# Two graph layers on one core: the attention weight as the larger of two exponentials, the second written to PSUM in pieces

## The reference

```python
# layer 0: maximum over the first 25 neighbours
h = jnp.maximum(_layernorm(x, axis=-1), 0.0)
vals, idx = jax.lax.top_k(scores, S)                 # S = 25, scores = -index where adj != 0
agg = feats.max(axis=2)                              # feats: the rows idx of h
x = x + relu(concat(h, agg) @ W + b)
# layer 1: attention
h = jnp.maximum(_layernorm(x, axis=-1), 0.0) @ W1
s1, s2 = h @ a1, h @ a2
e = jax.nn.leaky_relu(s1[:, :, None] + s2[:, None, :], negative_slope=0.4)
att = jax.nn.softmax(jnp.where(adj > 0, e, -1e+20), axis=1)
x = x + gelu(einsum('bij,bjo->bio', att, h))
```

## Time and profile before

| | |
|---|---|
| median of three runs | 4289.62 us |
| the profiled execution | 4290.73 us, span 4288.9 us |
| first and last gather start | 31.1 and 4116.5 us |
| DVE busy | 3346.5 us (78%) |
| POOL busy | 3107.7 us (72%) |
| PE busy | 2657.1 us (62%) |
| ACT busy | 1947.6 us (45%) |

### The profile page before, as it was taken

How to read it: one execution, slowest core, us unless ns; L and a number is a source line. 1 busy time by engine, 2 the same in 40 slices (tenths; PEclk the granted TensorE clock), 3 DMA queues, 4 the chain that set the end, 5 groups by cost and what they waited for, 6 DMA issues and landing times. The chain is left out here.

```text
span 4288.9 us, 43562 instructions
## 1 busy us (share of the span) xinstructions
PE 2657.1 (62%) x13568; PEld 2016.8 (47%) x13568; DVE 3346.5 (78%) x7253; ACT 1947.6 (45%) x2108; POOL 3107.7 (72%) x3205
## 2 busy tenths in 40 slices
PE   2333356666666666675676666666666666666669
PEld 2222234554445454454454554455445554454547
DVE  5666689966898669986799767996689876998656
ACT  4223255532665236642366335553255532664146
POOL 5777777777777777777777777777777777777730
PEclk8555557677777777777767777777776777677779
DMA  6555556666666766666666766666666666566531
GB/s 216 166 167 173 174 183 216 209 221 212 208 213 206 232 212 197 218 221 223 203 216 204 226 222 206 213 199 225 213 211 217 210 225 218 188 218 202 172 114 55
DMA packets 412749, 860.09 MB, mean 201 GB/s; under 512 B 67299, under 2 KB 248422, under 8 KB 396134
## 3 DMA queue, kind: packets, MB, share of 16 engines
q0 software_dynamic: 153600, 419.64, 32.0%
q1 hardware_dynamic: 258918, 437.67, 30.2%
HBM read 714.43 MB, written 142.61 MB: 200 GB/s over the span
## 5 line engine op out<-in xcount | busy, mean ns | idle before, releaser
L410 POOL DMA_INDIRECT gb<-h_table,idx x3200 | 3107.0, 971 | 1009.2 <-issue 962.2
L965 PE MATMUL ps_av<-hz,lk 128*128 128x256 f32 x3712 | 1136.1, 474 | 179.1 <-DVE hz L805 179.1
L965 PEld LDWEIGHTS ps_av<-hz,lk 128*128 128x128 f32 x3712 | 891.4, 247 | 418.9 <-issue 256.6
L724 DVE TENSOR_REDUCE hl<-gb 128x256 f32<-128x3328 f32 x128 | 740.8, 5787 | 401.6 <-DMA gb<-h_table,idx 401.2
L724 DVE TENSOR_REDUCE gb<-gb 128x256 f32<-128x3328 f32 x128 | 748.5, 5847 | 10.9 <-DMA gb<-h_table,idx 10.9
L1018 PE MATMUL ps_t<-cf,hl 128*128 128x128 f32 x512 | 121.1, 382 | 694.2 <-DVE hl L724 694.2
L1023 PE MATMUL ps_l<-w,hcat 128*128 128x256 f32 x1024 | 461.1, 628 | 86.5 <-ACT hcat L538 86.5
L538 ACT COPY hcat<-ps_t 128x512 f32<-128x512 f32 x128 | 74.9, 585 | 864.9 <-PE ps_t L1018 864.5
L1036 PE MATMUL ps_t<-cf,y 128*128 128x128 f32 x256 | 72.2, 375 | 586.7 <-ACT y L551 586.7
L1018 PEld LDWEIGHTS ps_t<-cf,hl 128*128 128x128 f32 x512 | 79.3, 192 | 740.8 <-issue 740.8
L426 ACT ACTIVATE sg<-ps_c 128x2048 bf16<-128x2048 bf16 x128 | 240.1, 1876 | 410.3 <-PE ps_c L942 399.3
(11 more groups left out here) (128 smaller groups left out, 3555.9 us busy)
## 6 DMA issues: line engine op xcount, KB each, us to landing
ad<-in_adj SPq DMA_DIRECT2D x128, 1024.0 KB
p_rest<-lk SPq DMA_DIRECT2D x112, 512.0 KB, 3.4
lk<-p_rest SPq DMA_DIRECT2D x112, 512.0 KB, 3.9
gb<-h_table,idx POOLq DMA_INDIRECT x3200
edges_t<-stage SPq DMA_DIRECT2D x32, 1024.0 KB, 7.1
edge<-edges_t SPq DMA_DIRECT2D x64, 512.0 KB, 7.0
xl<-in_x SPq DMA_DIRECT2D x128, 128.0 KB
hl<-h_table SPq DMA_DIRECT2D x128, 128.0 KB
```

What stands on the lines that cost most here:

```text
L410: pool.indirect_dma_start(gb[c][:, s + (c > 0), :], None, table[tb], bass.IndirectOffsetOnAxis(idx[u][:, k:k + 1], 0)).then_inc(gathered[c ...
L724: V.tensor_reduce(dst, gb[c][:, :, :].rearrange("p k c -> p c k"), AX.X, ALU.max).then_inc(maxed[c], 1)
L965: ins = T.matmul(accumulator(k), lk_of(jj, u, drain)[:, k * P:(k + 1) * P], hz[jj][:, :], start=False, stop=False)
```

## The change

With the bias b = nb, exp(leaky(v + s2) - bound) is the larger of exp(0.4 v + b) and exp(v + b + 0.6 s2), since the exponential keeps the order and leaky relu with slope 0.4 is the larger of two lines. The changed kernel makes both on ACT (`exps`) and the maximum of them on DVE (`item_max`). The first goes to SBUF as before, whole. The second goes in four pieces of 512 to `ps_n`, two banks used in turn; DVE reads a piece, takes the maximum, and writes the row sum of each piece to `z_p`. The bias of the first has `s2p` added, so `nb` has two parts and each item has its bounds right after its `val`. In the drain, where PE uses all banks, the second exponential goes over `val` in SBUF. `BLOCKED` becomes 2^100.

The two banks come from `ps_c`, which keeps one, and from `ps_t`, which becomes the same bank as `ps_l`. The signs are therefore transposed and read in two halves of 8 tiles over one bank.

```diff
-BLOCKED = 1e30
+BLOCKED = 2.0 ** 100
...
-        ps_c = ps("ps_c", [P, 1024], fp32)
-        ps_t = ps("ps_t", [P, 512], fp32)
+        ps_n = ps("ps_n", [P, 1024], fp32)
+        ps_c = ps("ps_c", [P, 512], fp32)
         ps_l = ps("ps_l", [P, 512], fp32)
+        ps_t = ps_l
...
-            def relu_part(i, j, jj, u, drain):
-                act.wait_ge(S["val_ready"], firsts(i) + 1)
+            def exps(i, j, jj, u, drain):
+
+                act.wait_ge(S["bounds_ready"], firsts(i) + 1)
                 act.wait_ge(S["av_done"], i - 2 if drain else i)
                 act.wait_ge(p_stored[jj], min(firsts(i) // 2, (NB - 1) * PAIRS) * 16)
-                nc.scalar.activation(lk_of(jj, u, drain)[:, :], val[jj][:, :], ACT.Relu, scale=1 - SLOPE,
-                                     bias=s2p[:, bass.ds(j, 1)]).then_inc(S["relu_ready"], 1)
-
-            def exp_part(i, j, jj, u, drain):
-                act.wait_ge(S["leaky_ready"], firsts(i) + 1)
-                bias, q = nb[:, bass.ds(j, 1)], lk_of(jj, u, drain)
-                nc.scalar.activation(q[:, :], q[:, :], ACT.Exp, bias=bias, accum_out=za[:, bass.ds(j, 1)]
-                                     ).then_inc(S["exp_ready"], 1)
+                nc.scalar.activation(lk_of(jj, u, drain)[:, :], val[jj][:, :], ACT.Exp, bias=nb[:, 1, bass.ds(j, 1)]
+                                     ).then_inc(S["exps_ready"], 1)
...
+                for p in range(0, N, PIECE):
+                    k = firsts(i) * (N // PIECE) + p // PIECE
+                    if k >= 2 and k % 4 == 1:
+                        act.wait_ge(S["p_ready"], k // 4)
+                    elif k >= 2:
+                        act.wait_ge(S["piece_read"], (k - 2) // 4 * 3 + (k - 2) % 4 + 1)
+                    nc.scalar.activation(ps_n[:, k % 2 * PIECE:(k % 2 + 1) * PIECE], val[jj][:, p:p + PIECE], ACT.Exp,
+                                         scale=SLOPE, bias=nb[:, 0, bass.ds(j, 1)]).then_inc(S["piece_ready"], 1)
...
                 if a:
-                    evacuate_signs(v + 4, (v + 4) % 8 * P)
+                    evacuate_signs(v + 4, (v + 4) % 8 * P, 0)
...
+                if a:
+                    evacuate_signs(v + 4, (v + 4) % 8 * P, 1)
...
-            def item_leaky(o, i, jj, u, drain):
+                V.tensor_tensor(nb[:, 1, bass.ds(j, 1)], nb[:, 0, bass.ds(j, 1)], s2p[:, bass.ds(j, 1)], ALU.add
+                                ).then_inc(S["bounds_ready"], 1)
+
+            def item_max(o, i, jj, u, drain):
...
                 for p in range(0, N, PIECE):
-                    ins = V.scalar_tensor_tensor(out=q[:, p:p + PIECE], in0=val[jj][:, p:p + PIECE], scalar=SLOPE,
-                                                 in1=q[:, p:p + PIECE], op0=ALU.mult, op1=ALU.add)
-                ins.then_inc(S["leaky_ready"], 1)
+                    k = firsts(i) * (N // PIECE) + p // PIECE
+                    dve.wait_ge(S["piece_ready"], k + 1)
+                    ins = V.scalar_tensor_tensor(out=q[:, p:p + PIECE], in0=q[:, p:p + PIECE], scalar=1.0,
+                                                 in1=ps_n[:, k % 2 * PIECE:(k % 2 + 1) * PIECE], op0=ALU.mult,
+                                                 op1=ALU.max, accum_out=z_p[:, jj, k % 4:k % 4 + 1])
+                    ins.then_inc(S["piece_read"] if p + PIECE < N else S["p_ready"], 1)
...
+                    n = o.mark(V.tensor_reduce(za[:, bass.ds(j, 1)], z_p[:, jj, :], AX.X, ALU.add))
...
             def transpose_signs(a):
                 pe.wait_ge(S["signed"], a + 1)
-                pe.wait_ge(S["edges_ready"], a)
                 pe.wait_ge(S["words_read"], a)
-                for m in range(TILES):
-                    ins = T.transpose(sgt[:, m * P:(m + 1) * P], sg[:, m * P:(m + 1) * P], identb)
-                ins.then_inc(S["signs_transposed"], 1)
+                for half in range(2):
+                    pe.wait_ge(S["edges_ready"], 2 * a + half)
+                    for m in range(PAIRS):
+                        ins = T.transpose(sgt[:, m * P:(m + 1) * P],
+                                          sg[:, (half * PAIRS + m) * P:(half * PAIRS + m + 1) * P], identb)
+                    ins.then_inc(S["signs_transposed"], 1)
...
+                    pe.wait_ge(S["h_saved"], v)
                     for k in range(4):
                         ins = T.transpose(ps_t[:, k * P:(k + 1) * P], hl[u][:, k // 2, k % 2 * P:(k % 2 + 1) * P], ident)
                     ins.then_inc(S["cat_transposed"], 1)
                     pe.wait_ge(S["cat_ready"], v + 1)
-                    pe.wait_ge(S["h_saved"], v)
```

More of the change, by code:

```diff
@@ L153, in graph_layers @@
         m_a = sb("m_a", [P, 2, 2], fp32)
-        nb = sb("nb", [P, TILES], fp32)
+        nb = sb("nb", [P, 2, TILES], fp32)
+        z_p = sb("z_p", [P, 2, N // PIECE], fp32)
         za = sb("za", [P, TILES], fp32)
@@ L511, in flush_last @@
                 act.wait_ge(S["sweep_done"], 2 * NB)
-                for k0, k1, accumulators in ((0, 4, ps_c), (4, 6, ps_t), (6, 8, ps_l)):
+                for k0, k1, accumulators in ((0, 4, ps_n), (4, 6, ps_c), (6, 8, ps_l)):
                     ins = nc.scalar.activation(go_last[:, k0:k1, :], accumulators[:, :].rearrange("p (k c) -> p k c", c=C),
@@ L529, in step @@
                     blocked(it, (b - 1) * 4 + i, 0, u, drain and t > 0)
-                if rest and not drain:
-                    exp_part(it - 2, j2, 0, 1 - u, drain)
                 if rest:
-                    relu_part(it - 1, j1, 1, 1 - u, drain and t > 0)
-                if rest and drain:
-                    exp_part(it - 2, j2, 0, 1 - u, drain)
+                    exps(it - 1, j1, 1, 1 - u, drain and t > 0)
                 if l:
@@ L552, in step @@
                                          ).then_inc(S["y1_ready"], 1)
-                if rest and not (drain and new):
-                    exp_part(it - 1, j1, 1, 1 - u, drain)
+                if a:
+                    evacuate_signs(v + 4, (v + 4) % 8 * P, 1)
                 if l:
@@ L559, in step @@
                 if start:
[L560 to L564, removed]
+                    exps(it, j, 0, u, drain)
                 if t == 0 and new:
@@ new lines, in item_bounds @@
+                dve.wait_ge(order, n)
+                V.tensor_tensor(nb[:, 1, bass.ds(j, 1)], nb[:, 0, bass.ds(j, 1)], s2p[:, bass.ds(j, 1)], ALU.add
+                                ).then_inc(S["bounds_ready"], 1)
+            def item_max(o, i, jj, u, drain):
+                q = lk_of(jj, u, drain)
+                dve.wait_ge(S["exps_ready"], firsts(i) + 1)
+                if i >= (NB - 1) * 32:
+                    n = (NB - 1) * TILES * (N // PIECE)
+                    dve.wait_ge(S["piece_ready"], n + firsts(i) - (NB - 1) * TILES + 1)
+                    for p in range(0, N, PIECE):
+                        k = p // PIECE
+                        ins = V.scalar_tensor_tensor(out=q[:, p:p + PIECE], in0=q[:, p:p + PIECE], scalar=1.0,
+                                                     in1=val[jj][:, p:p + PIECE], op0=ALU.mult, op1=ALU.max,
+                                                     accum_out=z_p[:, jj, k:k + 1])
+                    ins.then_inc(S["p_ready"], 1)
+                    return
+                for p in range(0, N, PIECE):
+                    k = firsts(i) * (N // PIECE) + p // PIECE
+                    dve.wait_ge(S["piece_ready"], k + 1)
+                    ins = V.scalar_tensor_tensor(out=q[:, p:p + PIECE], in0=q[:, p:p + PIECE], scalar=1.0,
+                                                 in1=ps_n[:, k % 2 * PIECE:(k % 2 + 1) * PIECE], op0=ALU.mult,
+                                                 op1=ALU.max, accum_out=z_p[:, jj, k % 4:k % 4 + 1])
+                    ins.then_inc(S["piece_read"] if p + PIECE < N else S["p_ready"], 1)
@@ L858, in step @@
                 if old and not drain and not before:
-                    item_leaky(o, it - 1, 1, 1 - u, drain)
-                if new and not t:
-                    take_s2(o, b)
+                    item_max(o, it - 1, 1, 1 - u, drain)
                 if words:
@@ L893, in step @@
                     item_value(o, it + 1, j + 1, 1, drain)
[L894 to L897, removed]
+                    item_bounds(o, it + 1, j + 1, 1)
                 if new and drain:
-                    item_leaky(o, it, 0, u, drain)
+                    item_max(o, it, 0, u, drain)
                 if old and t:
```

65 lines of the change are left out of this document (38 added, 27 removed).

## The result

The changed kernel takes 4534.0 us (four runs, 4529.06 to 4537.4) against 4290.28 us for four runs of the kernel before; the ratio is 1.0566, with a 95% interval from 1.0553 to 1.0579. The profiled execution has a span of 4527.3 us, 238.4 more than the 4288.9 before.

The account below looks back on a forecast made before the run. DVE and POOL were taken as bounds side by side in the attention half. +218 us in seven rounds, +1 at the start and +2 before the last flush, on the profiled 4290.7 us, gave 4510 us at the median (4440 to 4560).

Parts of the forecast that it names:

- The bounds: Attention half of a round: DVE's step of 32.04 us beside POOL's tile of 31.27; any microsecond added to DVE moves the end.
- The hold of `hcat`: ACT, attention steps: `hcat` waits behind pieces needing DVE's maximum; x1 at 17.0 instead of 12.46 us, +4.6 us a step.
- The rest of the cycle: DVE, attention step: x1 to the `gb` reduction 7.72 us, then 12.45 instead of 11.86; whole cycle 37.2 us.
- The size: Whole kernel: +218 us in seven rounds, +1 at the start, +2 ahead of the last flush, 221 in all.
- the excess of a round: Time of a round beyond POOL's tiles: 43.1 us after the change against 12.0 today, so +31.1 a round.
- the eight steps from one `gb` reduction to the other: DVE from step 0's `gb` reduction to step 8's in a round: 296.1 us, against POOL's 250.2.
- the lead of 2.8: DVE's lead over POOL in a round's attention steps, shrinking from 3.58 to 0.75 us; used up before POOL waits.
- the old excess: Kernel before: some 84 us beyond POOL's 128 tiles at 31.27 us, taken as 12.0 us in each of seven rounds.
- POOL's gain: Gathers beside DVE's sum: the maximum with one PSUM input would spare 42.9 us of lengthening, worth nothing while POOL awaits DVE.
- The halves: Signs in two halves on ACT and PE: hidden behind search and reduction, nothing in the steps, 1 us at the start.
- No change, if `hcat` weren't held: Rival, attention steps: only DVE's length counts, cycle 32.9 us, excess 12.0 as today, 4292 us; chance 0.04.
- Faster, POOL alone counts: Rival: POOL alone sets the time and the 42.9 us of gather lengthening vanish, 4251 us; chance 0.04.

Follow-up runs that it names:

- the first experiment: The changed kernel with ACT's copy of `hcat` moved between the second and third piece of the exponential: 4324.8 us, ratio 1.0070 to the kernel before.
- the third experiment: The changed kernel with DVE's maximum of item i-1 moved right after the `hl` reduction, ACT's order untouched: 4380.8 us, ratio 1.0204 to the kernel before.
- the last two: Kernel before with halves, ACT's relu in PSUM pieces, `hcat` between them, row sum on ACT: 4276.4 us; the same with rows of h scaled on ACT: 4267.9 us.
- the experiment with zeros: The kernel before with signs in halves, DVE's sum reading its second input from zeroed PSUM banks outside the drain (output wrong): 4260.1 us, ratio 0.9933.

## Why the prediction was right

The forecast was 4510 us (4440 to 4560), the measurement 4534.0.

- **The bounds.** DVE and POOL as bounds side by side in the attention half: right. DVE's cycle grew by some 5 us and the end moved by nearly as much in each step, while what POOL gained in its gathers (16 us) showed nowhere.
- **The hold of `hcat`.** Forecast: `hcat` at 11.7 and x1 at 17.0 us after the reduction starts. Measured over the 49 steps: 11.78 and 17.14 on average (in the step shown 2362.02 - 2350.26 = 11.76 and 16.91). That this hold is the loss, and not a neighbour of it, the first and the third experiment show from its two sides: moving either end of the wait, on ACT or on DVE, gives back 209 and 153 us.
- **The rest of the cycle.** x1 to `gb` 7.65 us in the step shown (forecast 7.72), `gb` to the next `hl` 12.40 (12.45), the whole 36.96 (37.2). A maximum with its accumulator and one input in PSUM costs 0.682 us and 0.61 from start to start, as assumed. ACT's pieces were undersized: 0.684 us each on the page, 1.30 for two, where I had taken 0.585 from a copy; the start to start is 0.62, so the sum hardly felt it.
- **The size.** The term that was low is the excess of a round, 31.1 forecast and 33.8 measured; seven times 2.7 us is 19 of the 24 us missing. The other 5 are no larger than the difference between the profiled execution, 4529.1 us, and the median of 4534.0. The DVE part of the excess, the eight steps from one `gb` reduction to the other, was 296.6 us on average and 296.1 in the sum. What I left out are the other eight steps: 249.1 us by the same reductions, where the sum has 250.2 less the lead of 2.8. I took the old excess for all sixteen, and of the new one only what DVE's cycle makes; but one gather at a round's head is still lengthened by 0.75 us beside the copy of `s1` (2209.51; the copy starts at 2209.18) and the one after it by 0.30 beside `val` (2211.52), and there are flushes and statistics beside. How the 1.7 us divide among these was not followed.
- **POOL's gain.** The maximum spares POOL entirely, as the rule of the Trainium skill has it ("SBUF — State Buffer", "Who interferes with whom"): 224 gathers began beside a maximum and none took over 1 us, where 100 of 224 did beside the sum. But only 24 of the 43 us went: the gathers over 1 us cost 56 us after and 80 before. (All gathers together are busy 16 us less, because the others ran a little longer.) The difference moved to `val`. Where POOL waited for the `gb` reduction, its first gather starts just behind it, where DVE does `val` with two SBUF inputs: 1.29 us at 2344.49, 1.28 at 2381.45. That was so in 43 of the 56 gathers that such a wait preceded, all 43 of them over 1 us, and they make 15 us. Beside `val` the lengthening rose from 19 to 40 us in all; the restart explains some 12 of these 21 us, and the rest wasn't followed. In this kernel it costs nothing, since POOL waits anyhow.
- **The halves.** Forecast 0 in the steps and 1 us at the start; alone they cost 0.0002 of the time, within what can be measured.
- **The rivals.** "No change, if `hcat` weren't held" was made real in the first experiment. It gave 4325 and not 4292, because DVE's list, the statistics of steps 6 and 7 included, is longer than POOL's tile. "Faster, POOL alone counts" came nearest in the last two, once DVE's list was about as short as before, with 0.55% and 0.74% (24 and 32 us) under the kernel before. The 42.9 us forecast for it were 30 us in the experiment with zeros (ratios 1.0002 and 0.9933).

## What to carry to other kernels

Before cutting an operation into pieces through two buffers, look at what stands behind it on the producing engine: from the third piece on the producer waits for the consumer, and everything behind inherits that wait. If the consumer later waits for any of it, it waits for itself; put the short, wanted copy between the second and the third piece. And where two engines are bounds side by side, a change that relieves one (here an operand in PSUM, worth about 30 us) pays only with a form that doesn't lengthen the other.

## What the runs showed that I had not expected

- A contention can move instead of vanish. With the maximum in PSUM the gathers lengthened beside `val` rose from 82 of 224 to 100 of 234, in part because POOL's restart fell into step with DVE.
- Writing 512 columns from SBUF to PSUM takes ACT 0.684 us and reading 512 from PSUM to SBUF 0.581; the first is an exponential and in the last variants a relu at 0.690, the second a copy. Which of the two differences makes the 0.1 us was not tried.
